# Three graph layers on one core: maxima, x low parts and the last norm placed elsewhere on VectorE, the second bias folded into other constants

## The reference

```
for l in range(3):
    scores = si[:, :, None] + sj[:, None, :] + attn_b[l]      # si, sj = x @ attn_w
    scores = where(scores >= 0, scores, 0.2 * scores)
    attn = softmax(where(mask, scores, -inf))
    h = layernorm(x + attn @ x) * g1[l] + beta1[l]
    ff = gelu(h @ W1[l] + b1[l]) @ W2[l] + b2[l]
    x = layernorm(h + ff) * g2[l] + beta2[l]
out = layernorm(x1 + x)                                        # x1: what the layers got
```

## Time and profile before

| | us |
|---|---|
| median of 3 runs | 2741.6 |
| lowest, highest | 2737.8, 2743.8 |
| profiled execution | 2739.8 |
| its span | 2737.9 |
| mean granted clock of TensorE over the span | 0.956 |

### The profile page before, as it was taken

One profiled execution on the slowest core, in us unless ns is written; L12 is line 12 of the kernel. 1 busy time (PEld: TensorE's weight loads), 2 busy tenths in 40 slices (PEclk: granted clock), 3 DMA queues, 4 the chain that ended last, 5 costly groups with the idle time before them and its releaser, 6 DMA issues.

```text
span 2737.9 us, 45987 instructions
## 1 busy us (share of the span) xinstructions
PE 2442.5 (89%) x16548; PEld 2240.7 (82%) x16548; DVE 2374.1 (87%) x5832; ACT 1706.6 (62%) x2682; POOL 520.5 (19%) x501
## 2 busy tenths in 40 slices
PE   8999999945999999999899999999988898988895
PEld 6999999935888888888788888888878787878785
DVE  5888888877999899999889999999988888888774
ACT  3444444434777677677676777676766666665752
POOL 3555555510010010010000100100101011101010
PEclk9999999977999999999999999999999999898997
DMA  4444444444223133233232332322323332322111
GB/s 145 137 139 142 138 142 139 141 105 121 63 84 91 49 85 82 74 86 85 78 93 70 86 86 56 84 82 74 93 72 95 81 89 66 89 82 78 47 32 39
DMA packets 349492, 247.72 MB, mean 90 GB/s; under 512 B 213712, under 2 KB 308304, under 8 KB 349264
## 3 DMA queue, kind: packets, MB, share of 16 engines
q1 hardware_dynamic: 349264, 244.78, 31.7%
HBM read 144.07 MB, written 50.33 MB: 71 GB/s over the span
## 4 chain that ended last, share of the span: by engine, by line
PE 37%; DVE 29%; issue 6%; ACT 4%; DMA 1%; POOL 1%; SPq 1%; ACTq 0%; DVEq 0%; POOLq 0%
PE G L43 5%; PE G L45 5%; PE G L44 5%; DVE spare L1076 5%; DVE pT_lo L1112 4%; PE Y L1405 4%; PE Y L1406 4%; PE Y L1407 4%; DVE prod L1183 3%; PE A L1365 3%; PE A L1366 2%; PE A L1367 2%; DVE u L1124 2%; DVE xo L1169 2%; DVE xo L1162 2%
## 5 line engine op out<-in xcount | busy, mean ns | idle before, releaser
L993 ACT ACTIVATE g<-G,b 128x512 f32<-128x512 f32 x384 | 264.0, 688 | 561.5 <-PE G L45 441.7
L1365 PE MATMUL A<-x_hi,pT_hi 128*128 128x258 f32 x1536 | 464.1, 302 | 147.7 <-DVE pT_lo L1112 147.5
L1405 PE MATMUL Y<-w_hi,g_hi 128*128 128x256 f32 x1536 | 441.4, 287 | 69.0 <-DVE g_lo L1203 69.0
L1366 PE MATMUL A<-x_hi,pT_lo 128*128 128x258 f32 x1536 | 450.5, 293 | 0.0
L1367 PE MATMUL A<-x_lo,pT_hi 128*128 128x256 f32 x1536 | 448.9, 292 | 0.0
L1365 PEld LDWEIGHTS A<-x_hi,pT_hi 128*128 128x128 f32 x1536 | 308.4, 201 | 164.0 <-issue 142.7
L1406 PE MATMUL Y<-w_lo,g_hi 128*128 128x256 f32 x1536 | 431.0, 281 | 0.0
L1407 PE MATMUL Y<-w_hi,g_lo 128*128 128x256 f32 x1536 | 430.5, 280 | 0.0
L1203 DVE TENSOR_TENSOR g_lo<-g,g_hi 128x512 fp32r<-128x512 f32 x384 | 263.0, 685 | 138.0 <-ACT g_hi L996 137.6
L1405 PEld LDWEIGHTS Y<-w_hi,g_hi 128*128 128x128 f32 x1536 | 291.3, 190 | 92.5 <-DVE g_lo L1203 83.9
L43 PE MATMUL G<-h_hi,w_hi 128*128 128x512 f32 x768 | 310.6, 404 | 10.0 <-DVE h_lo L1198 10.0
(11 more groups left out here) (172 smaller groups left out, 5873.6 us busy)
## 6 DMA issues: line engine op xcount, KB each, us to landing
mask<-mask SPq DMA_DIRECT2D x192, 256.0 KB, 3.0
a_adj_t<-in_adj SPq DMA_DIRECT2D x64, 512.0 KB, 4.0
x_rows<-rows SPq DMA_DIRECT2D x24, 1024.0 KB, 6.1
mask<-a_mask SPq DMA_DIRECT2D x64, 256.0 KB, 4.3
rows<-xo SPq DMA_DIRECT2D x32, 512.0 KB, 2.9
a_xs<-in_x SPq DMA_DIRECT2D x9, 1024.0 KB, 9.9
x_rows<-in_x SPq DMA_DIRECT2D x8, 1024.0 KB, 7.8
rows<-a_xo SPq DMA_DIRECT2D x64, 128.0 KB, 3.7
```

The source lines that it names most:

```text
L1365: pe.matmul(L.A[:, t, 0:DE], hi, L.x_hi[:, par, j, :], start=(j == 0), stop=False)
L1366: pe.matmul(L.A[:, t, 0:DE], lo, L.x_hi[:, par, j, :], start=False, stop=False)
L1405: pe.matmul(L.Y[:, t, :], hi, L.w2[0][:, f, :], start=False, stop=False)
```

## The change

On VectorE: of the four maxima of a step one stays ahead of `h_lo`, one goes to f = 3, one to f = 5 and one in front of `p_lo(k+1, 0)`. The x low parts go from f = 3 and 4 to f = 4 and 6, as one instruction over two tiles instead of two. `final` is split: `final_stats` stands where `projections` do in other layers, `final_norm` at f = 1. On SP the store is issued at one place in all layers, and on GpSimd the final deviation comes ahead of the first norm's.

The second bias goes: h is kept with b2 added (`shift` = beta1 + b2), so the residual brings b2 along, and the product with W1 is corrected by b1 - W1 b2 (`b1_less`). TensorE computes W1 b2 once per layer in `fold_b2`, VectorE subtracts it in `less_b2`. `share`, its products and b2's wide loads go; b2 comes as columns.

```diff
-                for dst, src in ((L.b1, b1), (L.g1, g1), (L.be1, be1)):
+                for dst, src in ((L.b1, b1), (L.g1, g1), (L.be1, be1), (L.b2, b2)):
...
-                if k >= 2 and layer_of(k - 2) < LAYERS - 1:
+                if k >= 2:
                     store(k - 2)
...
-                if k < K:
-                    deviation1(k)
                 i = k - 2 - (K - C)
                 if i >= 0:
                     deviation2(L.s_fin_mv, TC * (i + 1), L.s_fin_rs, i)
+                if k < K:
+                    deviation1(k)
...
+            def less_b2(layer):
+
+                dve.wait_ge(L.s_fold, layer + 1)
+                folded = L.Y[:, 0, 0:2 * KF].rearrange("p (f i) -> p f i", i=2)
+                dve.scalar_tensor_tensor(L.b1_less[:, layer, :], folded[:, :, 0], -1.0, L.b1[:, layer, :], ALU.mult,
+                                         ALU.add).then_inc(L.s_b1, 1)
...
                 if projected:
                     projections(k - 2)
+                elif old:
+                    final_stats(k - 2)
+                if ffn and new_layer(k - 1):
+                    less_b2(layer_of(k - 1))
                 if agg:
                     norm1(k)
...
+                    if f == 1 and old and not projected:
+                        final_norm(k - 2)
...
-                    if f in (3, 4) and k + 2 < K:
-                        for t in (0, 1) if f == 3 else (2, 3):
-                            x_lo(k + 2, t)
+                    if f in (4, 6) and k + 2 < K:
+                        x_lo(k + 2, f // 2 - 2)
+                    if f in (3, 5):
+                        for r in tops[f // 2:f // 2 + 1]:
+                            row_top(r)
                     if f >= 4 and agg and new_layer(k):
                         weights_lo(layer_of(k), f - 4)
-                    if f == 5:
-                        for r in tops[1:2]:
-                            row_top(r)
                 if after:
                     add_mask(k + 1, KF - 1)
-                if old and not projected:
-                    final(k - 2)
...
-                if after:
-                    p_lo(k + 1, 0)
-                for r in tops[2:3]:
+                for r in tops[3:]:
                     row_top(r)
...
+            def fold_b2(layer):
+
+                m = C * layer
+                pe.wait_ge(L.s_w_lo, 2 * KF * (layer + 1))
+                pe.wait_ge(L.s_b2, 2)
+                if m >= 1:
+                    pe.wait_ge(L.s_n2, TC * m)
+                for f in range(KF):
+                    for part in range(2):
+                        for i in range(KD):
+                            mm = pe.matmul(L.Y[:, 0, 2 * f:2 * f + 2], L.w1[part][:, i, f * P:(f + 1) * P], L.b2_parts[:, layer, i, :],
+                                           start=(f == 0 and part == 0 and i == 0), stop=(f == KF - 1 and part == 1 and i == KD - 1))
+                mm.then_inc(L.s_fold, 1)
...
                     transpose_n1(k - 1)
+                if ffn and new_layer(k - 1):
+                    fold_b2(layer_of(k - 1))
                 if ffn:
                     up(k - 1, 0)
```

More of the change, by code:

```diff
@@ L646, in layer_buffers @@
     L.ident = sb("ident", [P, P])
-    L.share = sb("share", [P, P], F32R)
     L.half = sb("half", [P, TC])
@@ L857, in _ @@
                 load_maskT(0, half)
-            for layer in range(LAYERS):
-                sp.dma_start(L.xo[:, layer, :], b2[layer].partition_broadcast(P)).then_inc(L.s_b2_in, 16)
             for r in range(MASKS, NT):
@@ L906, in _ @@
             pool.memset(L.eps[:, :], EPS).then_inc(L.s_consts, 1)
-            pool.memset(L.share[:, :].bitcast(F32), 2.0 / P).then_inc(L.s_ones, 1)
             for i in range(2):
@@ L977, in h @@
                 for dst in (L.h, L.h_hi):
-                    act.activation(dst[:, i, :], L.G[i][:, :], ACT.Identity, bias=L.be1[:, layer, i:i + 1],
+                    act.activation(dst[:, i, :], L.G[i][:, :], ACT.Identity, bias=L.shift[:, layer, i:i + 1],
                                    scale=L.g1[:, layer, i:i + 1]).then_inc(L.s_h, 1)
@@ L988, in gelu @@
                 n = KF * m + f
-                bias = L.b1[:, layer_of(m), f:f + 1]
+                bias = L.b1_less[:, layer_of(m), f:f + 1]
+                if new_layer(m) and f == 0:
+                    act.wait_ge(L.s_b1, 2 * (layer_of(m) + 1))
                 act.wait_ge(L.s_ffn1, n + 1)
@@ L1184, in projections, with x_lo @@
                                                  accum_out=L.uv[:, slot, i, t:t + 1]).then_inc(L.s_uv, 1)
-            def x_lo(j, t):
-                par, s = j // 2 % 2, TC * (j % 2) + t
-                if t == 0:
+            def x_lo(j, half):
+                par, s = j // 2 % 2, TC * (j % 2) + 2 * half
+                if half == 0:
                     dve.wait_ge(L.s_x_hi, j + 1)
-                mm = dve.tensor_tensor(L.x_lo[:, par, s, :], L.x[:, par, s, :], L.x_hi[:, par, s, 0:D].bitcast(F32), ALU.subtract)
-                if t == TC - 1:
-                    mm.then_inc(L.s_x_lo, 1)
+                dve.tensor_tensor(L.x_lo[:, par, s:s + 2, :], L.x[:, par, s:s + 2, :], L.x_hi[:, par, s:s + 2, 0:D].bitcast(F32),
+                                  ALU.subtract).then_inc(L.s_x_lo, 1)
+            def less_b2(layer):
[3 more added lines that the diff above has]
+                                         ALU.add).then_inc(L.s_b1, 1)
+                dve.wait_ge(L.s_b1, 2 * layer + 1)
+                dve.scalar_tensor_tensor(L.b1_less[:, layer, :], folded[:, :, 1], -1.0, L.b1_less[:, layer, :], ALU.mult,
+                                         ALU.add).then_inc(L.s_b1, 1)
             def h_lo(m):
@@ L1204, in g_lo, with final_stats @@
                                   ALU.subtract).then_inc(L.s_g_lo, 1)
-            def final(m):
+            def final_stats(m):
                 i = m - (K - C)
@@ L1240, in _ @@
             for j in range(2):
-                for t in range(TC):
-                    x_lo(j, t)
-            dve.wait_ge(L.s_b2_hi, 1)
-            for layer in range(LAYERS):
-                low = slice(P // 2, P)
-                dve.tensor_tensor(L.b2[low, layer, :], L.xo[low, layer, :], L.b2[low, layer, :].bitcast(F32),
-                                  ALU.subtract).then_inc(L.s_b2_done, 1)
+                for half in range(2):
+                    x_lo(j, half)
+            dve.wait_ge(L.s_columns, 16 * 4 * LAYERS)
+            dve.tensor_copy(L.b2_parts[:, :, :, 0], L.b2[:, :, :]).then_inc(L.s_b2, 1)
+            dve.wait_ge(L.s_b2, 1)
+            dve.tensor_tensor(L.b2_parts[:, :, :, 1], L.b2[:, :, :], L.b2_parts[:, :, :, 0].bitcast(F32),
+                              ALU.subtract).then_inc(L.s_b2, 1)
+            dve.tensor_tensor(L.shift[:, :, :], L.be1[:, :, :], L.b2[:, :, :], ALU.add).then_inc(L.s_b2, 1)
             for j in range(LEAD):
@@ L1315, in _ @@
                         weights_lo(layer_of(k), f)
-                for r in tops[3:]:
-                    row_top(r)
         @block.tensor
@@ L1370, in residual @@
             def residual(m):
-                if m == 0:
-                    pe.wait_ge(L.s_b2_done, LAYERS)
-                else:
+                if new_layer(m):
+                    pe.wait_ge(L.s_b1, 2 * (layer_of(m) + 1))
+                elif m >= 1:
                     pe.wait_ge(L.s_n2, TC * m)
-                for c in range(2):
-                    pe.matmul(L.Y[:, 2 * c:2 * c + 2, :], L.share[:, :], L.b2[:, layer_of(m), :].unsqueeze(1).to_broadcast([P, 2, D]),
-                              start=True, stop=False)
                 for t in range(TC):
                     for i in range(KD):
-                        pe.matmul(L.Y[:, t, i * P:(i + 1) * P], L.h[:, i, t * P:(t + 1) * P], L.ident[:, :], start=False, stop=False,
-                                  is_transpose=True)
+                        pe.matmul(L.Y[:, t, i * P:(i + 1) * P], L.h[:, i, t * P:(t + 1) * P], L.ident[:, :],
+                                  start=(t % 2 == 0 and i == 0), stop=False, is_transpose=True)
+            def fold_b2(layer):
+                m = C * layer
+                pe.wait_ge(L.s_w_lo, 2 * KF * (layer + 1))
+                pe.wait_ge(L.s_b2, 2)
+                if m >= 1:
+                    pe.wait_ge(L.s_n2, TC * m)
[5 more added lines that the diff above has]
+                mm.then_inc(L.s_fold, 1)
             def up(m, f):
```

39 lines of the change are left out of this document (18 added, 21 removed).

## The result

| | before | after |
|---|---|---|
| median, us (4 runs each, same chip) | 2739.68 | 2659.47 |
| lowest, highest | 2734.6, 2743.8 | 2657.8, 2660.4 |
| span of the profiled execution | 2737.9 | 2657.7 |
| granted clock of TensorE over the span | 0.956 | 0.976 |

A forecast was written before the change was run, and what follows sets the result against it. It took VectorE's head and TensorE's feed-forward part in series as the bound, ScalarE's exps beside the head. Terms -7.3 - 10.7 - 63 - 11 + 5.5 + 3 - 2.4 = -85.9 from 2739.8 gave 2653.9, about 2655 us; range 2640 to 2677.

The forecast's parts named there:

- the likeliest case: Whole kernel: the forecast itself, about 2655 us, given 75% against its rivals.
- step 0: start, weights: Kernel start: b2's DMAs gone before the masks -1.5, less x and b2 work -0.9; weights about 1 us later.
- Steps 18, 19 and 34: Around layer changes: the maxima's 0.25 us gain counted for 19, no maxima gain for 18 and 34.
- The weights' +3: Steps 0, 16, 32: maxima ahead of weights_lo free the weights' buffer about 1 us later each; +3 (0 to +6).
- The maxima: VectorE's head, 29 steps: one maximum less gains 0.25 us, not 1.15, because p_lo wait for ScalarE's exps; -7.3.
- The clock: Seven slow steps (3, 7, 8, 9, 27, 28, 29): TensorE's half-clock stretches disappear; -10.7, or 0 at the other end.
- The rival that the sum of idleness counts: TensorE: summed idleness, not the longest gap, lowers the clock, so stretches stay; +10.7 to +21, 2666 to 2676 us; 12%.
- The gap ahead of the first down product: TensorE, each step: idleness shrinks from 2.07 to 1.3 us, covering the later aggregation.
- The last layer and the tail: Steps 35 to 47 become normal steps, 528 us against 591.1, -63; after them the final norm and store waits shrink, -11.
- The fold: Steps 1, 17, 33: 32 two-column products before up(0); +2.9 in step 1, 1.3 each later, +5.5 (to +14).

The follow-up runs named there:

- the second profile: The changed kernel run again unaltered, on the same chip as three other follow-up kernels: 2659.1 us, ratio 0.9705.
- the run with one exp: The changed kernel without the second of ScalarE's two exps for each j, low parts computed from the logits: 2600.4 us, ratio 0.949.
- the three repairs: Changed kernel plus second norm's vectors loaded early, small gelu before the folded-bias wait, less_b2 inside norm1: 2661.1 us; with the new buffer declared last, 2653.3.
- the two last repairs: Small gelu before the folded-bias wait and less_b2 inside norm1, added to the changed kernel with early vector loads: 2653.3 us against 2651.7, buffer declared last.

## Why the prediction was right, and where it was off

The range held, and the likeliest case is what happened; the median is 4.5 us above the forecast. By the stamps of GpSimd in the first profile of either kernel, term by term:

| us | predicted | measured |
|---|---|---|
| step 0: start, weights | -1.4 | -4.8 |
| step 1: fold | +2.9 | +3.8 |
| steps 2 to 16: maxima, four clock stretches | -9.9 | -9.7 |
| steps 17, 33: fold, and the weights' 2 us forecast for 16, 32 | +4.6 | +1.8 |
| steps 18, 19 | -0.25 | +3.6 |
| steps 20 to 32: maxima, three stretches | -7.9 | -7.9 |
| step 34 | 0 | +5.8 |
| steps 35 to 47 | -63 | -62.3 |
| tail | -11 | -10.5 |
| sum | -85.9 | -80.2 |

That the sum came so near is partly luck. Steps 18, 19 and 34 cost 9.7 us more than forecast, and the start and the weights gave 6 of these back in this profile, by no merit of the terms (in the second profile steps 17 and 33 take 1.6 more). At the start 1.4 us lie in the first stage, which the change doesn't touch (VectorE's `ub` starts at 588.77 before and 587.38 after), and VectorE's wait for a mask is 0.84 in place of 3.77, where 1.5 less was forecast. The weights' +3 is a term that no run measured apart; steps 16 and 32 have the normal 40.2.

*The maxima.* The step of the argument that mattered was not to count the 1.15 us of the instruction but to follow the p_lo against ScalarE's pace. It gave p_lo(2), p_lo(3) and p_lo(6) 1.45, 2.70 and 6.38 behind the start of p_lo(0); they stand at 1.48, 2.71 and 6.40 (1418.70 to 1420.18, 1421.41, 1425.10). The steps gained 0.23 and 0.29. That it is ScalarE is shown by the run with one exp: another 1.2 us a step. Of these 0.9 are the waits; where the other 0.3 come from was not followed.

*The clock.* Taken as gone, and gone. The rival that the sum of idleness counts has fallen: the changed kernel idles 1.55 + 1.57 in a step, more than the 0.63 + 2.07 of before, and no normal step has a half-clock stretch in either of its profiles; the maxima alone (1.59 + 1.1) show none either, while before, final norm alone and fold alone (0.6 + 2.1 to 2.5) show two to eight each. But no length of gap parts the two cases. The last layer's steps have gaps of 1.95 now, and in the kernel with the early loads the clock fell behind four of them, at no cost to the step (37, clock 0.96, 41.14 us). With the three repairs it fell once behind 1.77, and that step, 39, took 42.80 in place of 41.28 (timeline of TensorE, table of stretches):

```profile
2227.56 0.44 PE L1425 MATMUL Y<-w_hi,g_hi 128*128 128x256 f32 x1 [1.77 <-DVE g_lo L1211]
```
```profile
2228.00:2231.00 3.00, 3.00 (x14) 2.81 (x14) 2.87 (x9) 1.81 (x3) 0.68 (x1) 0.50 0.00 0
```

And gaps of 2.1 to 2.5 were followed by a fall only now and then. This is where the Trainium skill (TensorE: Matmul & The Clock Gate, "A second HAM failure mode: psum-queue depth-cycling") has frequent short idles between groups enough to make the clock oscillate; in these traces two pauses of 1.6 us in every normal step did not. The size, 10.7, was the count of one execution. The runs of the kernel before lie 18 us apart on one chip, and a part of its time is the luck of that count.

*The gap ahead of the first down product* was put at 1.3, the 0.47 of the removed b2 products included, and is 1.57; where these products stay, with the maxima alone, it is 1.12 to 1.20. The 0.3 between was not followed. It cost nothing.

*The last layer and the tail* came as worked out: 40.34 and 41.15 a step in steps 36 to 44. The sum over steps 35 to 47 holds two half-clock stretches, in 35 and 46, which the cheaper steps 45 and 47 (39.70 and 38.90) mostly make up for. One thing the sum did not see: it relied on having the maxima beside it, and without the final norm out of the way they would have cost there.

*Steps 18, 19 and 34* are the miss, 9.7 us. Two causes. First, step 34 was not in the sum. It is the first with a final norm; before, that stood at its end, behind the stamp, and the step had no projections either, which made it the cheapest of all (40.19). Now 2.9 us of sum and statistics stand inside it. That could have been read ahead of the run; my boundary, "steps 35 to 47", was drawn one step late. Second, the wait for the second norm's vectors was taken to be as it was. The loads are issued at the end of the step before, behind three masks and ahead of a chunk of x. The later of the two (at 1374.60) landed 7.4 us after its issue where it had taken 6.2, and that 1.2 is all that step 18 got longer. In step 34 the landing came 1.6 later behind an issue that was itself 1.2 later, and with the 3.0 of the final norm these make its 5.8. So these steps are as long as the load lets them be, and a gain of VectorE's ahead of it is worth nothing there. Why the landing was later stays open: in the second profile it took 6.6 and 6.5. The rest, step 19, is a half-clock stretch, which the second profile doesn't have there and the final norm alone does; that part is luck. Loading the vectors early took off 9.2 us against the first profile, 6.5 against the second.

*The fold.* 32 matmuls from 678.90 to the first of up(0) at 682.39 are 3.49 us, 109 ns each; the nearest row had said 0.108 and 3.5. The Trainium skill's 81 ns for a pair of weight load and 128-column matmul (TensorE: Matmul & The Clock Gate, "Back-to-back issue gap") would have made an estimated 2.6; the trace, with two columns a matmul, disagrees.

```profile
678.90 0.28 PE L1397 MATMUL Y<-b_parts,w_hi 128*128 128x2 f32 x2
...
682.39 0.48 PE L43 MATMUL G<-h_hi,w_hi 128*128 128x512 f32 x1
```

What the term left out is the clock. In the kernels with the fold TensorE falls to half clock 2 to 5 us behind the start of a fold, for some 4 or some 7 us, in 28 of the 30 folds of their ten profiles, with no pause over 0.25 us in the 5 us ahead of the fold. In the repeated run of the early loads, step 17, the fold starts at 1341.33, TensorE is busy all through, and the clock is 1.00 and then 0.50 (table of stretches):

```profile
1341.30:1343.30 2.00, 2.00 (x21) 2.00 (x19) 1.97 (x6) 0.00 (x0) 0.00 (x0) 1.00 0.39 123
1344.00:1350.00 6.00, 6.00 (x21) 5.13 (x21) 5.59 (x27) 1.01 (x1) 0.00 (x0) 0.50 0.62 130
```

Step 1 shows it best: with the fold nine of ten profiles have the stretch, and of the four without it (before, final norm alone, maxima alone, fold left out) none does at that place. The one exception with the fold is the profile that the table above is made from. In the second profile of the changed kernel, with the stretch, steps 1 and 2 take 87.8 in place of 85.7: that the table's row for step 1 is only +3.8, and step 2 no longer than forecast, is luck as well. Steps 17 and 33 have a stretch without the fold too, behind another gap (3.03 us with the fold left out). It may be part of why the two last repairs bring nothing: with both, and a stretch of 7 us, steps 1 and 2 take 88.0.

The new wait on ScalarE, with the table load behind it, was not seen in the diff. It may be the 0.9 us by which step 1 exceeds its term in this profile. Its price was not measured apart from the rest.

## What to carry to other kernels

Before crediting a moved instruction with its duration, lay the next engine's pace beside it: here 1.15 us became 0.25, with each wait within 0.03 us of where the rows put it. Before crediting a gain per step to every step, look at the first and last step of each phase: where a step ends with the landing of a load, a faster engine gains nothing. Before explaining a difference of 3 us in one or two steps, take a second profile: of the 3.6 in steps 18 and 19 only 0.4 was left in it. And two edits that look independent may need each other; the maxima alone gained some 4 us, since in the last layer they lost 9.6 of the 17 that they had gained in the normal steps.

## What the runs showed of the hardware that was not expected

- An unused buffer of 48 bytes a partition, declared in the midst of others, made the kernel 9 us slower (2668.4 against 2659.1; 5 of them in every profile, by 0.08 and 0.14 us a step): the down matmuls follow each other at 120.0 in place of 117.7 ns. Declared last, a buffer of the same size did not. A change that adds or removes a buffer can move the time by this alone, and an experiment that adds one should declare it last.
- The clock also fell without a pause close ahead of it: in or right behind the 32 matmuls of two columns each, which followed each other at 109 ns, TensorE went from 2.4 to 1.2 GHz in 28 of 30 cases, for some 4 or 7 us. Steps 1 and 2, where the fold stands, took 85.7 us in the one profile without such a stretch, 86.0 and 86.5 in two with 4 us of it, and 87.3 to 88.0 in five with 7.
- With one wait more ahead of a gelu, the load of its table, 1.28 us, no longer ran right behind the last instruction of the old table (681.42 in the kernel before) but only when both waits were over (684.11).
- The clock makes executions of one program differ: 19 runs of the kernel before on one chip lie 18 us apart (2729.1 to 2746.9), the fastest at a mean clock of 0.961 and the slowest at 0.953. Four runs of the changed kernel lie 5 apart (2656.1 to 2660.7), which is too few to call its spread smaller.
